# An adaLN feed-forward layer on one core: branch products of three batches deferred to the ending, and the last batch's y term accumulated onto x in the output

## The reference

```python
c = einsum('bsi,boi->bso', x, weight[ids])            # 2048 x 2048 for each of 8 batches
c_norm = c * rsqrt(mean(c * c, -1) + eps)
H_res = sinkhorn_log(((c_norm @ W_res.T) + base_res) / 0.1, 50 steps)   # 4 x 4 per token
H_pre = softmax(c_norm @ W_pre.T + base_pre)          # 4 per token
H_post = softmax(c_norm @ W_post.T + base_post)       # 4 per token
H_res = (1 - g) * I + g * H_res
y = einsum('btjc,btj->btc', streams(c), H_pre) @ W_branch               # 512 x 512
out = x + einsum('btij,btjc->btic', H_res, streams(c)) + y (x) H_post
```

## Time and profile before

| | |
|---|---|
| median of 3 runs | 1706.34 us (1702.9 to 1706.88) |
| the profiled execution | 1707.7 us, of which the profile's span is 1705.9 us |
| end of the last batch's products | about 1598 us |
| busy in the span: TensorE, VectorE, ScalarE | 1686.9, 1425.8, 711.7 us |
| DMA | 252.41 MB, mean 148 GB/s |

### The profile page before, as it was taken

One profiled execution on the slowest core, in us unless ns is written; L12 is line 12 of the kernel. 1 busy time (PEld: TensorE's weight loads), 2 busy tenths in 40 slices (PEclk: granted clock), 3 DMA queues, 4 the chain that ended last, 5 costly groups with the idle time before them and its releaser, 6 DMA issues.

```text
span 1705.9 us, 24515 instructions
## 1 busy us (share of the span) xinstructions
PE 1686.9 (99%) x7748; PEld 1362.3 (80%) x7748; DVE 1425.8 (84%) x5973; ACT 711.7 (42%) x1161; POOL 99.0 (6%) x139
## 2 busy tenths in 40 slices
PE   9999999999999999999999999999999999999998
PEld 7888888887888878888788878888788877888774
DVE  4322499988998889988899979998899898998798
ACT  4333534244334343434334344333533444335562
POOL 0000000010000100001000000001000010001121
PEclk9999999999999999999999999999999999999999
DMA  6323423475243832358325573346632593227888
GB/s 241 97 87 124 148 91 108 111 217 183 95 112 112 255 140 93 107 146 272 100 87 124 167 229 104 107 112 196 197 101 87 142 300 138 90 91 205 229 165 209
DMA packets 68865, 252.41 MB, mean 148 GB/s; under 512 B 7936, under 2 KB 8064, under 8 KB 67840
## 3 DMA queue, kind: packets, MB, share of 16 engines
q1 hardware_dynamic: 49584, 181.11, 32.7%
q0 software_dynamic: 19152, 69.74, 17.3%
HBM read 203.63 MB, written 42.99 MB: 145 GB/s over the span
## 4 chain that ended last, share of the span: by engine, by line
PE 85%; DVE 10%; DMA 3%; ACT 1%; issue 1%; SPq 0%; DVEq 0%; ACTq 0%
PE acc L1231 73%; PE y_ps L1310 3%; PE turn_ps L1268 3%; DMA piece<-xn 3%; DVE piece L1083 2%; PE logit_ps L1276 2%; PE logit_ps L1279 2%; DVE vec L1019 1%; DVE vec L1017 1%; DVE work L1021 1%; DVE w_lo L834 1%; DVE x_lo L842 1%; DMA w_raw<-wt 1%; PE acc L1257 1%; PE y_ps L1300 1%
## 5 line engine op out<-in xcount | busy, mean ns | idle before, releaser
L1231 PE MATMUL acc<-w_hi,x_hi 128*128 128x512 f32 x2032 | 804.7, 396 | 1.0 <-ACT acc L532 1.0
L1231 PE MATMUL acc<-w_hi,x_lo 128*128 128x512 f32 x2032 | 792.8, 390 | 0.0
L1231 PE MATMUL acc<-w_lo,x_hi 128*128 128x512 f32 x2032 | 791.3, 389 | 0.0
L499 ACT ACTIVATE w_hi<-w_raw 128x1024 fp32r<-128x1024 f32 x255 | 269.5, 1058 | 454.3 <-DMA w_raw<-wt 454.3
L1231 PEld LDWEIGHTS acc<-w_hi,x_lo 128*128 128x128 f32 x2032 | 381.3, 188 | 82.1
L1231 PEld LDWEIGHTS acc<-w_hi,x_hi 128*128 128x128 f32 x2032 | 381.7, 188 | 80.6 <-DVE w_lo L834 1.5
L1231 PEld LDWEIGHTS acc<-w_lo,x_hi 128*128 128x128 f32 x2032 | 382.0, 188 | 76.5
L834 DVE TENSOR_TENSOR w_lo<-w_raw,w_hi 128x1024 fp32r<-128x1024 f32 x256 | 311.7, 1217 | 134.2 <-ACT w_hi L499 124.7
L1083 DVE SCALAR_TENSOR_TENSOR piece<-cond,kern,piece 128x512 f32<-128x512 f32 x416 | 282.9, 744 | 7.8 <-DMA piece<-xn 7.8
L1019 DVE RECIPROCAL vec<-vec 128x8 f32<-128x8 f32 x1536 | 240.1, 198 | 0.0
L1017 DVE TENSOR_REDUCE vec<-work 128x8 f32<-128x32 f32 x1536 | 237.7, 194 | 0.2
(11 more groups left out here) (172 smaller groups left out, 841.8 us busy)
## 6 DMA issues: line engine op xcount, KB each, us to landing
w_raw<-wt SPq DMA_DIRECT2D x255, 512.0 KB, 3.6
x_raw<-xt SPq DMA_DIRECT2D x63, 512.0 KB, 5.7
out<-piece POOLq DMA_DIRECT2D x58, 512.0 KB, 4.7
piece<-xn POOLq DMA_DIRECT2D x56, 512.0 KB, 7.2
grouped<-cond SPq DMA_DIRECT2D x16, 256.0 KB, 9.9
out<-cond POOLq DMA_DIRECT2D x8, 512.0 KB, 7.0
out<-x_raw SPq DMA_DIRECT2D x7, 512.0 KB, 2.6
out<-late_own POOLq DMA_DIRECT2D x6, 512.0 KB, 9.8
```

The source lines that it names most:

```text
L499: nc.scalar.activation(w_hi[:, unit % HI_SLOTS, :, :], w_raw[:, unit % LO_SLOTS, :, :], ACT.Copy).then_inc(w_hi_ready, 1)
L1231: mm = nc.tensor.matmul(acc[t][:], stationary, moving, start=(chunk == 0 and m == 0), stop=(chunk == CHUNKS - 1 and m == 2))
```

## The change

`LATES` becomes 3 and `FIRST_LATE` 4: batch 4 is late too. Its `turn_pre`, `branch` and their high and low parts leave the loop and come in the ending as tiles 8 to 11; `kept` has two planes, stored at the start of batches 6 and 7, and loaded into two halves of `w_raw`. A third pair of parts (`third_t`) and a fourth bank serve the late tiles.

For batch 7 the matmuls with `y_block`, `copy_y`, `copy_base` and `add_end` go. During batch 7 SP copies x from the input to the output in DRAM, eight transfers of 512 KB. `spread_last` writes y times post to a slot, as for a late tile, and `add_base` adds it to the output with four accumulating transfers of 256 KB per tile (32 partitions each, rows of 2 KB). Then `load_base` loads x + post y of the tile, 1 MB, to `end_out`, where VectorE adds the mixing matmul and SP stores as before, now in plain order. All 16 tiles (12 late, 4 of batch 7, numbers 12 to 15) go through 6 slots of 1 MB each in the order `SPREAD_ORDER`. The lists of the three engines are rewritten.

```diff
@@ constants
-LATES = 2
+LATES = 3
 FIRST_LATE = BATCHES - 1 - LATES
-LATE_OWN, LATE_SLOTS = 3, 11
-COPIED = 10
+LATE_SLOTS = 6
+X_COPIED_AT = (2, 5, 8, 11, 14, 17, 20, 23)
+SPREAD_ORDER = (0, 1, 2, 3, 12, 4, 5, 13, 6, 7, 8, 14, 15, 9, 10, 11)
+def added_count(s):
+    return sum(2 * 16 for i in range(s % LATE_SLOTS, s + 1, LATE_SLOTS)
+               if SPREAD_ORDER[i] < LATE_TILES)
...
@@ SyncE
+            def load_base(tile):
+                place = (BATCHES - 1) * MIX_PAIRS + 2 * tile
+                sp.wait_ge(base_added[tile], GROUPS * 16)
+                sp.dma_start(end_out[:, tile * GROUPS:(tile + 1) * GROUPS, :]
+                             .rearrange("p (q e) c -> p q (e c)", e=2),
+                             out[place:place + 2, :, :].rearrange("q p f -> p q f")
+                             ).then_inc(base_loaded[tile], 16)
...
             def ending():
-                load_last_residual(MIX_PAIRS - 1)
                 sp.wait_ge(acc_done, BATCHES * STREAMS * TILES)
-                sp.wait_ge(late_kept, 16)
-                sp.dma_start(late_x, kept.rearrange("p (t c) -> p t c", t=TILES)
-                             ).then_inc(late_back, 16)
+                sp.wait_ge(late_kept, (LATES - 1) * 16)
+                load_kept(1)
                 for j in range(STREAMS):
                     group_cond(j)
-                for n in MIX_ORDER[0:END_PLANES - 2:2]:
-                    store_planes(n, 2)
-                for n in MIX_ORDER[END_PLANES - 2:]:
-                    store_planes(n, 1)
+                for late in range(2, LATES):
+                    load_kept(late)
+                for tile in range(TILES):
+                    load_base(tile)
+                for q in range(MIX_PAIRS - 1):
+                    store_planes(2 * q, 2)
+                for e in range(2):
+                    store_planes(END_PLANES - 2 + e, 1)
...
-                    if last and U == 0:
-                        sp.wait_ge(pre_ready, (FIRST_LATE + 1) * TILES)
+                    if end and b > FIRST_LATE + 1 and U == 0:
+                        sp.wait_ge(pre_ready, (b - 1) * TILES)
+                        sp.dma_start(kept[b - 2 - FIRST_LATE, :, :] ...
+                    if last and U in X_COPIED_AT:
+                        place = (BATCHES - 1) * MIX_PAIRS + X_COPIED_AT.index(U)
+                        sp.dma_start(out[place, :, :], xn[place, :, :]).then_inc(x_copied, 16)
@@ POOL: add_late by tile (two transfers of 512 KB), and in place of add_end
+            def add_base(tile):
+                s = SPREAD_ORDER.index(LATE_TILES + tile)
+                pool.wait_ge(late_spread, (s + 1) * STREAMS)
+                pool.wait_ge(x_copied, MIX_PAIRS * 16)
+                for g in range(GROUPS):
+                    place = (BATCHES - 1) * MIX_PAIRS + 2 * tile + g // 2
+                    cols = slice(g % 2 * C, (g % 2 + 1) * C)
+                    nc.gpsimd.dma_start(out[place, :, cols].rearrange("(i k) c -> k i c", k=GROUP),
+                                        late_out[s % LATE_SLOTS][g * GROUP:(g + 1) * GROUP, :, :],
+                                        accum_op=ALU.add).then_inc(base_added[tile], 16)
@@ ScalarE: spread_post, copy_y, copy_base go
+                def spread(k, bank, weight):
+                    s = SPREAD_ORDER.index(k)
+                    if s >= LATE_SLOTS:
+                        previous = SPREAD_ORDER[s - LATE_SLOTS]
+                        if previous < LATE_TILES:
+                            act.wait_ge(late_added[s % LATE_SLOTS], added_count(s - LATE_SLOTS))
+                        else:
+                            act.wait_ge(base_added[previous - LATE_TILES], GROUPS * 16)
+                    for i in range(STREAMS):
+                        nc.scalar.activation(late_out[s % LATE_SLOTS][:, i, :], bank[:], ACT.Copy,
+                                             scale=weight[:, i:i + 1]).then_inc(late_spread, 1)
...
+                def spread_last(t):
+                    act.wait_ge(y_ready, first_tile + t + 1)
+                    spread(LATE_TILES + t, y_ps[t % 2], logit[:, t, NRES + STREAMS:NLOGIT])
@@ ScalarE's list: seven spreads ahead of the second logarithmic step
                 spread_late(4)
                 late_low(5)
                 late_high(6)
                 pre_high(1)
                 spread_late(5)
                 pre_low(1)
                 late_low(6)
                 answer_log_step(asks, 1)
@@ VectorE
                     def add_base(n):
-                        bank = end_bank[MIX_ORDER.index(n) % len(end_bank)]
-                        if n < COPIED:
-                            dve.wait_ge(end_added[n // 2], 16)
-                        else:
-                            dve.wait_ge(x_in[n // 2], (BATCHES + 1) * 16)
+                        dve.wait_ge(base_loaded[n // GROUPS], 16)
+                        dve.wait_ge(block_mixed, n + 1)
@@ TensorE: y_product, sum_base, keep_base go
                 def branch_late(k):
-                    if k > 2:
-                        pe.wait_ge(late_spread, (k - 2) * STREAMS)
-                    multiply(late_parts[k % 2], acc[k % 3]).then_inc(late_y_ready, 1)
+                    if k >= TILES:
+                        place = SPREAD_ORDER.index(k - TILES)
+                        pe.wait_ge(late_spread, (place + 1) * STREAMS)
+                    multiply(late_parts[k % 3], acc[k % TILES]).then_inc(late_y_ready, 1)
...
                 def mix_group(n):
+                    t, bank = n // GROUPS, end_bank[n % len(end_bank)]
+                    pe.wait_ge(mix_block_ready, t + 1)
+                    if n == 1:
+                        places = [SPREAD_ORDER.index(LATE_TILES + k) for k in (2, 3)]
+                        pe.wait_ge(late_spread, (max(places) + 1) * STREAMS)
+                    if n == 3:
+                        pe.wait_ge(late_spread, (LATE_TILES + TILES) * STREAMS)
+                    if n >= len(end_bank):
+                        pe.wait_ge(out_ready, n - len(end_bank) + 1)
```

More of the change, by code:

```diff
@@ L415, in _ @@
             for slot in range(LATE_SLOTS):
[L416 removed]
+                sp.wait_ge(late_added[slot], added_count(max(
+                    range(slot, LATE_TILES + TILES, LATE_SLOTS))))
             sp.wait_ge(stored_last, (MIX_PAIRS + 1) * 16)
@@ L441, in store @@
                                     ).then_inc(stored[q % OUT_SLOTS], 16)
[L443 to L460, removed]
+            def add_late(k):
+                late, tile = divmod(k, TILES)
+                s = SPREAD_ORDER.index(k)
+                for p in range(2):
+                    q = 2 * tile + p
+                    place = (BATCHES - 2 - late) * MIX_PAIRS + q
+                    pool.wait_ge(late_spread, s * STREAMS + 2 * (p + 1))
+                    pool.wait_ge(stored[q % OUT_SLOTS], (place // OUT_SLOTS + 1) * 16)
+                    nc.gpsimd.dma_start(out[place, :, :].rearrange("p (s c) -> p s c", s=2),
+                                        late_out[s % LATE_SLOTS][:, 2 * p:2 * p + 2, :],
+                                        accum_op=ALU.add
+                                        ).then_inc(late_added[s % LATE_SLOTS], 16)
@@ L472, in _ @@
             store(BATCHES - 2, MIX_PAIRS - 1)
[L473 to L487, removed]
+            add_late(0)
+            add_late(1)
+            add_late(2)
+            add_late(3)
+            add_base(0)
+            add_late(4)
+            add_late(5)
+            add_base(1)
+            add_late(6)
+            add_late(7)
+            add_late(8)
+            add_base(2)
+            add_base(3)
+            add_late(9)
+            add_late(10)
+            add_late(11)
         @block.scalar
@@ L567, in spread_pre @@
                     for j in range(STREAMS):
[L568 to L582, removed]
+                        nc.scalar.activation(pre_diag[:, t, j, :], ident[:], ACT.Copy,
+                                             scale=logit[:, t, NRES + j:NRES + j + 1]
+                                             ).then_inc(pre_spread, 1)
                 def late_high(k):
@@ L1372, in turn_late @@
                         cols = slice(m * P, (m + 1) * P)
-                        mm = nc.tensor.matmul(late_turn[k][:, cols], (xpre, late_x)[late][:, t, cols],
+                        mm = nc.tensor.matmul(late_turn[k][:, cols], ([xpre] + late_x)[late][:, t, cols],
                                               ident[:], start=(m == 0), stop=(m == C // P - 1),
@@ new lines, in ending @@
+                turn_late(5)
+                branch_late(4)
+                turn_late(6)
+                take_late(5)
+                weigh_and_turn(1)
+                branch_late(5)
+                take_late(6)
+                take_pre(1)
+                turn_late(7)
+                weigh_and_turn(2)
+                branch_last(1)
+                branch_late(6)
+                take_late(7)
+                take_pre(2)
```

(4 more changed lines are left out.)

280 lines of the change are left out of this document (109 added, 171 removed).

## The result

The changed kernel takes 1719.71 us (median of 4, 1717.66 to 1721.79) against 1706.61 for the kernel before (median of 4). The ratio of the two is 1.0081, 95% interval 1.0062 to 1.0101: 0.8% slower. The profiled execution took 1718.93 us, of which the span is 1716.7, 10.8 us more than before. One execution of all those reported here, of the run with regrouping on two queues, took 2052.71 us at a granted clock of 0.77 and is left out of its numbers.

What follows compares the result with a forecast made beforehand. TensorE was taken to bound the loop and filled DMA engines the changed ending: last product at 1587.7 us plus 140.7 us of engine time gives a 1728.4 us span, forecast as 1729 us, range 1714 to 1748.

Steps and rivals of the forecast that it cites:

- the ledger: Ending: DMA engine time summed by queue, 97.0 us before, +43.7 us from the change, 140.7 us in all.
- the packing: Ending: shares up to 3% over 1 (-4 us) cancel the last transfer's landing with small gaps (+4 us).
- The loop's saving: Loop over batches: without batch 4's products the last product ends 10.3 us sooner, 12.7 us kept for the range.
- The 2 KB rows: Ending: sixteen 256 KB accumulations of post times y cost the same per byte as 4 KB rows, +23.2 us.
- rival 1: Ending: 2 KB rows cost up to double, +23.2 us, 1752 us, halfway 1740; chance 0.22 for over 1740.
- Rival 2: Ending: POOL's and SP's DMA queues overlap, so POOL's alone decides, 1700 us; chance 0.08.
- Rival 3: Ending: accumulations cost what stores do, 1.3 us each, so the chain ends it at 1696 us; chance 0.03.
- Costed at nothing: Batches 6 and 7: second `kept` store and eight copies of x, 10 to 23 us engine time, add nothing.
- ScalarE before the second logarithmic step: Ending: ScalarE may answer VectorE late there, some 2 us, in a chain that has slack.
- The waiting spread that just fits: Ending: ScalarE's last spread waits for a slot, is over at 89 us, when the mixing starts.
- The claim that POOL's queue does not run dry: Ending: tiles are spread every 4 to 6 us, engines need 5.8 us each, so POOL's queue stays fed.
- The signs: Trace marks of a right forecast, among them ending DMA share 0.95 or more, POOL's queue 0.18 to 0.19 MB per filled us.

## Why the prediction was right

The direction and the mechanism were right: work moved off TensorE into an ending whose DMA engines were filled, and the engines' ledger set the end. The size was not: the span grew by 10.8 us where 22.5 were forecast, half. The time, 1719.7 us, lies 9 us below the 1729 forecast, inside the range of 1714 to 1748. Three terms erred the same way: the start of the ending by 2.2 us, the ledger by 4.7, the packing by 4.8. Point by point:

- *What bounds.* TensorE in the loop: its products left, and the interval shortened by 11.96 us. In the ending the DMA engines: shown by the run with plain stores (-1.2%, no order changed) and the one with half of the base transfers.
- *The loop's saving* was mis-sized. I took 10.3 us from the comparison of two intervals rather than the 12.7 of the instruction count. In the profiled pair it is 12.5, over all traces 11.7, between the two. The interval of 193.48 that I compared with is the longest of its kind; it holds the wait of 1.0 us for ScalarE in the earlier trace rows, which is shorter or missing in the other traces. Against the 192.1 that this interval takes in the mean of the other five kernels with two late batches, 203.81 would have given 11.7.
- *The ledger.* Forecast 140.7 us, measured by the same reading, stage by stage: POOL's queue 0.7 + 9.6 + 17.2 + 14.2 + 14.3 + 16.8 + 10.8 + 3.6 = 87.2 us, SP's 20.2 + 7.0 + 2.8 + 2.8 + 0.7 + 6.0 + 9.3 = 48.8, together 136.0. SP's part (47.6 forecast) fits. POOL's was 92.8: the 2.90 us per 512 KB, read in stages with other traffic and outliers, were too dear; 86.5 us of accumulation for 16.8 MB are 2.70 us. The accumulated rows of 4 KB have a median of 328 ns in both endings, but before the change single ones took up to 2.7 us, and their mean was 359, after it 328.
- *The packing.* I let 4 us of shares over 1 cancel against 4 us for gaps and the last landing. The first had the right size: 136.0 us of engine time stood in the 131.2 us from 1585.5 to 1716.7, a mean of 1.04. The second had no row behind it, and the trace shows none of it as a net loss. Together with the ledger and the start (1585.5, not 1587.7) this makes up the 11.7 us between the 1728.4 forecast for the span and 1716.7.
- *The 2 KB rows* pay nearly by the byte (178 ns beside 328), as taken; the double price of rival 1 falls. The reason that I gave, a row that is only partly on the narrow side, no run shows.
- *Rival 2*, queues that overlap, falls: with both at work, 67.5% and 37.8% make 105%, and the shares over 1 are 4 to 10 per cent. *Rival 3* would have needed accumulations at the price of stores; the run that gave this price to the 24 of 512 KB ended near where it said, at 1698.6 us against 1696. By the Trainium skill's fit in "DMA: Bandwidth & Descriptors", section "Anatomy of one DMA — SWDGE (gpsimd) path", I estimate 1.2 us for the bytes of a 512 KB transfer, its fixed 2 us left out. The plain stores come near that, with 8 rows of 159 ns per engine or 1.3 us; the accumulations, at 2.70, do not.
- *Costed at nothing*: the copies of x, shown by doubling them. ScalarE before the second logarithmic step: it waited up to 1.15 us for VectorE there, not the other way. The waiting spread that just fits: the last one waited 4.7 us for its slot and was over at 1673.2, before the first mixing matmul at 1675.15.
- *The claim that POOL's queue does not run dry* held because SP's regrouping covers the time until the first late tile. The run with the regrouping moved away showed how much hangs on that: 6 of the 11 us became a hole.
- *The signs.* Two were missed by little: the share of the last stage is 0.86, not 0.95, and POOL's queue moved 0.194 MB per filled us, where I had written 0.18 to 0.19.

What deferring batch 4 trades is thus some 12 us of TensorE in the loop for 8 accumulations and a load, some 24 us on engines that were full, with the 11 us of room already taken by the new y term. The difference of the two is close to the 11 us by which the run with two late batches is faster.

## What to carry to other kernels

Before work is moved to a stage "beside the critical path", add up that stage's DMA time by queue, with accumulating bytes at their own price (2.1 to 2.2 times a store here): the engine that is free by its busy share is not the one that the moved work uses. A sum of engine time gives the end only if the queue is fed from the first moment; time freed before the first item is ready turns into a hole, and transfers moved into a busy stage can hold up that stage's own. And the difference of two intervals of one trace has a scatter (here up to 1.6 us between executions for the same work): set the count of instructions, or more traces, beside it.

## What the runs showed of the hardware that was not expected

Shares of the DMA engines above 1 are not only rounding: 1.04 to 1.10 over the six stages of 16 us from 1606 us, highest in the two with most accumulated rows of 2 KB (1.08, there POOL's queue alone with 107.5%, and 1.10). Why a sum of packet times can exceed the engines' time stays open. An accumulated row of 4 KB takes 328 ns, a stored one 159. A copy of 32 partitions inside SBUF takes 635 ns per row of 8 KB, twice that store per byte, whether one queue or two issue it. TensorE's granted clock fell from 1.00 to 0.50 at 1683.1 us, 2.1 us after the last of 64 back to back matmuls, when only some of the eight small spreading matmuls came in between; in the kernel before, the same gap was passed at 0.95 or more and the clock was down, at a mean of 0.61, only in 1688 to 1692 us, with TensorE at work on the mixing:

```profile
1683.00:1685.00 2.00, 1.61 (x10) 0.97 (x8) 0.68 (x4) 0.00 (x0) 0.00 (x0) 1.00 1.04 190
1685.00:1688.00 3.00, 1.33 (x3) 0.73 (x4) 2.18 (x5) 0.00 (x0) 0.00 (x0) 0.95 1.04 203
1688.00:1692.00 4.00, 4.00 (x7) 1.61 (x6) 2.54 (x4) 0.00 (x0) 0.00 (x0) 0.61 0.28 103
```

Why the fall comes later there stays open.
